# Attention with experts behind it: denominators apart from values, the out projection opened early, the next batch's norm and half of the slots moved

## The chip, the cores and the metric

One core of a Trainium2 chip runs the kernel. Its engines are TensorE (PE: matrix products and transposes), VectorE (DVE), ScalarE (ACT), GpSimd (POOL) and SyncE (SP, which issues most transfers). The metric is the time of one execution on the device in microseconds (us).

## The reference

Cut to what matters. Four batches of 512 tokens, 256 features; 64 context rows each; 16 heads of 16 features; 8 experts with 1024 hidden features, 2 per token.

```python
def xattn(Q, K, V, ...):               # Q = layernorm(x), K = V = context
    q, k, v = Q @ Wq + bq, K @ Wk + bk, V @ Wv + bv          # split into 16 heads
    A = softmax(scale * einsum("blhe,bshe->bhls", q, k))
    return einsum("bhls,bshd->blhd", A, v).reshape(B, L, H * E) @ We + be
x = x + xattn(layernorm(x), context, ...)
def ffn(x, ...):                       # x = layernorm(x)
    probs = softmax(x @ router_w + router_b)
    top_w, top_idx = top_k(probs, 2)
    comb = sum(top_w[..., None] * one_hot(top_idx, E), axis=1)
    for e in range(E):
        out += comb[:, e] * (gelu(x @ up[e].T) @ down[e].T)
x = x + ffn(layernorm(x), ...)
```

## The kernel before, in words

The kernel has two stages. The attention stage takes the batches one after the other and also routes the tokens: for each token it finds two experts and a slot in a table. The expert stage, behind it, gathers rows by that table, multiplies them with the experts' weights and adds them to the output. The change touches the attention stage only.

Products that must keep float32 precision are done in three: the left side and the right side are each split into a high half (ACT copies it, rounded) and a low half (VectorE subtracts the high half from the source), and PE multiplies high by high, high by low and low by high (`three`, L1253). So nearly each product waits for an ACT copy and a VectorE subtraction.

Each engine has its own queue, written out by hand, and executes it in order; semaphores hold it where it needs another's result. An engine's `batch(i)` works on three batches at once: the scores of batch i, the second half of the softmax, the out projection and the router logits of batch i-1, and the slots of batch i-2.

PE's queue for one batch (L1471): values and denominators of heads 0 to 7 of batch i-1 (`values`, four j, L1339); half of batch i's normed rows turned (`x_turn`); turned scores j = 4..7 (`scores_turned`); the other `x_turn`; values and denominators of j = 4..7; `project_q(i)`, first k = 1 and then k = 0; the denominators turned (`den_turn`); counts for the slots (`positions`); scores in four parts with the turned reciprocals (`rden_turn`) and their spread over the features (`spread`) between them; `project_out(i-1)`; the maxima turned (`max_turn`); turned scores j = 0..3; the second norm's rows turned (`x2_turn`); `slots` half 0; router logits; their transpose; `slots` half 1.

`values` writes, for each j, a product of 32 columns into bankA and one into bankB0, in the quarter j % 4 of the output partitions. The profile shows products of different quarters starting within 0.02 us of each other. bankB0 (which is also bank 3 of bankC) serves in turn for the denominators, q (k = 0), the first half of the out projection and the router logits; bankB1 for x_turn, q (k = 1) and the second half of the out projection.

VectorE's queue for one batch (L1001): `norm1` of batch i (normed rows xn); `low01` (low halves of expert weights, two operations); `x_low` half 0; `router` of batch i-2 (probabilities, the two best); `x_low` half 1; `chosen` (masks); `q_low` twice; own counts; `rden_split` (reciprocals of the denominators and their halves); the score maxima in four parts, with `att` (attention output times reciprocal) and `att_low` (its low half, at_l) between them; `max_split`; `ranks` and `count`; `residual_norm2` of batch i-1, which ends with the rows xr; `puts` (eight pairs hot/put for the slots); `logits`.

ACT makes the high halves, the exponentials (`exps`) and copies out of PSUM (`av_copy`, `den_copy`, `x2_turn`, `logit_copy`). POOL makes block forms of the keys (`key_blocks`, L381), four operations per batch that wait for the last turned score; the powers for the norms (`rstd`); and the value blocks.

Behind the loop comes the rest of the last batch: values, slots of batch 2, a few products of zeros (`keep_busy`) between short steps, the out projection and the first expert products. `low01` of the last batch stands on VectorE's queue ahead of `residual_norm2`.

## Time and profile before

| | us |
|---|---|
| median of 3 runs | 405.82 |
| lowest and highest | 405.77, 406.33 |
| the profiled execution | 406.0 |
| its span, first to last instruction | 403.5 |
| PE busy | 370.9 (92%) |
| VectorE busy | 242.4 (60%) |
| ScalarE busy | 180.1 (45%) |
| POOL busy | 159.0 (39%) |
| mean granted clock of PE | 0.988 of full |

Busy times are of one engine each and overlap. A line of the profile gives the engine, the line of the kernel, the tile written and those read, the shape, and in brackets how long the engine was idle before it and what ended the wait. The busy time of matrix products is modelled and includes their overlap with the next, so the distance from start to start says what a product takes: 0.23 us for 512 columns, 0.12 for 256.

### The profile page before, as it was taken

How to read it: one execution, taken by the hardware profiler on the slowest of the kernel's cores; microseconds unless marked ns; L12 is line 12 of the kernel's file. 1: busy time of each engine (PE TensorE's matmuls, PEld its weight loads, DVE VectorE, ACT ScalarE, POOL GpSimd, SP SyncE). 2: the span in 40 equal slices, each digit the busy share in tenths (PEclk: the TensorE clock that was granted, in tenths of full speed). 3: DMA queues.
4: the chain of work that ended last, by engine and by line, in shares of the span. 5: the costliest groups of instructions: out<-in, count | busy, mean ns of one | idle time of the engine just before them, and what ended most of it. 6: DMA issues, size and time to landing. Idle time of an engine off the chain costs nothing.

```text
span 403.5 us, 8452 instructions
## 1 busy us (share of the span) xinstructions
PE 370.9 (92%) x2521; PEld 326.4 (81%) x2522; DVE 242.4 (60%) x693; ACT 180.1 (45%) x283; POOL 159.0 (39%) x186
## 2 busy tenths in 40 slices
PE   8998988998898888989889999999999999999990
PEld 8775667576566656988889999999999999999990
DVE  4267596789979975878334366574747447342440
ACT  1263544444444424643325557465474274262340
POOL 2043402212040204115454683846648718616522
PEclk9999999999999999998999999999999999999996
DMA  8910301041031111155232373937556522312322
GB/s 271 352 72 1 106 0 53 2 158 54 0 105 54 53 55 54 54 155 162 42 57 26 66 226 78 251 92 202 169 105 210 106 25 53 56 23 45 49 24 26
DMA packets 26389, 37.23 MB, mean 92 GB/s; under 512 B 4705, under 2 KB 17441, under 8 KB 26369
## 3 DMA queue, kind: packets, MB, share of 16 engines
q1 hardware_dynamic: 19312, 26.98, 20.2%
q0 software_dynamic: 7056, 9.99, 14.3%
q8 instruction: 11, 0.18, 0.2%
q14 instruction: 10, 0.07, 0.1%
HBM read 27.18 MB, written 9.79 MB: 92 GB/s over the span
## 4 chain that ended last, share of the span: by engine, by line
PE 73%; DVE 15%; issue 5%; POOL 3%; ACT 3%; DMA 1%; DVEq 0%; POOLq 0%; ACTq 0%
PE bankC L1255 10%; PE bankC L1257 10%; PE bankC L1256 10%; PE bankD L1619 7%; PE bankD L1620 6%; PE bankD L1621 6%; DVE nmax L798 3%; PE bankC L1454 3%; PE bankA L1587 2%; PE bankA L1349 2%; PE bankC L1619 2%; PE bankC L1450 2%; PE bankC L1620 1%; PE bankC L1621 1%; POOL rstd L374 1%
## 5 line engine op out<-in xcount | busy, mean ns | idle before, releaser
L700 ACT ACTIVATE hh<-bankC 128x512 fp32r<-128x512 f32 (+1 forms) x52 | 36.3, 697 | 93.3 <-PE bankC L1257 93.3
L1255 PE MATMUL bankC<-xnT_h,up_w 128*128 128x256 f32 (+1 forms) x240 | 74.5, 310 | 2.0 <-ACT prime L694 1.4
L1256 PE MATMUL bankC<-xnT_l,up_w 128*128 128x256 f32 (+1 forms) x240 | 72.9, 304 | 0.0
L1257 PE MATMUL bankC<-xnT_h,up_w 128*128 128x256 f32 (+1 forms) x240 | 72.8, 303 | 0.0
L1619 PE MATMUL bankD<-dn_w,hh 128*128 x208 | 59.9, 288 | 0.9 <-issue 0.5
L1620 PE MATMUL bankD<-dn_w,hh 128*128 x208 | 58.3, 280 | 0.5 <-issue 0.5
L1621 PE MATMUL bankD<-dn_w,hl 128*128 x208 | 58.1, 279 | 0.0
L450 POOL DMA_INDIRECT xr<-rows,idx_g x35 | 47.3, 1353 | 14.8 <-issue 14.0
L1182 DVE TENSOR_TENSOR hl<-prob,hh 128x512 fp32r<-128x512 f32 (+1 forms) x26 | 21.2, 816 | 46.1 <-ACT prob L701 46.1
L1255 PEld LDWEIGHTS bankC<-xnT_h,up_w 128*128 128x128 f32 x240 | 45.5, 190 | 2.9 <-ACT prime L694 1.6
L1256 PEld LDWEIGHTS bankC<-xnT_l,up_w 128*128 128x128 f32 x240 | 45.7, 191 | 0.0
L1257 PEld LDWEIGHTS bankC<-xnT_h,up_w 128*128 128x128 f32 x240 | 45.6, 190 | 0.0
L1619 PEld LDWEIGHTS bankD<-dn_w,hh 128*128 128x128 f32 x208 | 39.0, 188 | 3.6 <-issue 2.8
L1621 PEld LDWEIGHTS bankD<-dn_w,hl 128*128 128x128 f32 x208 | 39.1, 188 | 0.6 <-issue 0.6
L1620 PEld LDWEIGHTS bankD<-dn_w,hh 128*128 128x128 f32 x208 | 39.1, 188 | 0.0
L374 POOL TENSOR_TENSOR rstd<-var,cst 128x2 f32<-128x2 f32 (+2 forms) x10 | 9.6, 958 | 65.2 <-DVE var L862 58.0
L1182 DVE TENSOR_TENSOR hl<-raw,hh 128x512 fp32r<-128x512 f32 (+1 forms) x26 | 21.2, 815 | 23.3 <-ACT raw L701 23.3
L418 POOL TENSOR_TENSOR prime<-prime 1x1 f32<-1x1 f32 x39 | 12.1, 309 | 58.5 <-DVE gate L1169 49.2
L455 POOL DMA_INDIRECT out<-x2T,idx_s x18 | 29.7, 1648 | 6.1 <-issue 6.1
L1255 PE MATMUL bankC<-hh 128*128 128x512 f32 x64 | 26.8, 419 | 3.2 <-ACT nmxT L557 2.8
L566 ACT ACTIVATE prob<-bankC 128x512 f32<-128x512 f32 x32 | 19.1, 598 | 15.3 <-PE bankC L1337 15.3
L455 POOL DMA_INDIRECT out<-av,idx_s x14 | 24.1, 1718 | 3.6 <-issue 3.6
(312 smaller groups left out, 866.9 us busy)
## 6 DMA issues: line engine op xcount, KB each, us to landing
xall<-up SPq DMA_DIRECT2D x24, 256.0 KB, 3.8
xall<-down SPq DMA_DIRECT2D x24, 256.0 KB, 4.2
rows<-xr SPq DMA_DIRECT2D x4, 528.0 KB, 3.3
raw<-up SPq DMA_DIRECT2D x4, 512.0 KB, 4.7
raw<-down SPq DMA_DIRECT2D x4, 512.0 KB, 5.3
out<-xall SPq DMA_DIRECT2D x4, 512.0 KB, 2.8
xall<-x SPq DMA_DIRECT2D x1, 1536.0 KB, 8.2
cst<-const SPq DMA_DIRECT2D x1, 640.0 KB, 8.2
```

What stands on the lines that cost most here:

```text
L374: return g.tensor_tensor(out_, var_, c("power")[:, 0:n], ALU.pow)
L450: return g.indirect_dma_start(xr[:, t, :], None, rows, bass.IndirectOffsetOnAxis(idx_g[:, n:n + 1], 0), bounds_check=T + P - 1)
L455: g.indirect_dma_start(out, bass.IndirectOffsetOnAxis(idx_s[:, n:n + 1], 0), y[ring][:, t, :], None, bounds_check=T + P - 1, compute_op=AL ...
L566: a.activation(prob[:, j % 4, :], bankC[:, j % 3, :], ACT.Exp, scale=SCALE).then_inc(a_exp, 1)
L700: a.activation(hT_h[:, 2 * q:2 * q + 2, 0:n * P], bank, ACT.Gelu)
L1182: v.tensor_tensor(hT_l[:, 2 * q:2 * q + 2, 0:n * P], hbuf[q][:, :, 0:n * P], hT_h[:, 2 * q:2 * q + 2, 0:n * P].bitcast(F32), ALU.subtract) ...
L1255: mm(out_, left_h, right_h, start=first, stop=False)
L1256: mm(out_, left_h, right_l, start=False, stop=False)
L1257: return mm(out_, left_l, right_h, start=False, stop=last)
L1619: mm(out_, hT_h[:, m, o], w_h, start=(m == 0), stop=False)
L1620: mm(out_, hT_h[:, m, o], w_l, start=False, stop=False)
L1621: last = mm(out_, hT_l[:, m, o], w_h, start=False, stop=(m == KF - 1))
```

## The change

All of it is in the order of the queues and in what is waited for; no product and no operation is added or taken away.

- Out projection: the offset products of both halves come first, without a wait for the low half; the high halves follow after a wait for `a_at`, the low halves last after `v_at`.
- Turned scores, j = 0: the wait for the turned maxima moves from ahead of the three score products to ahead of the product that adds the maxima.
- `values` becomes `weighted` and `denominator`. For j = 0..3 the weighted values stand at the end of the batch ahead of the logits, the denominators last; x_turn of the next batch stands between the logits and their transpose. For j = 4..7 they stay together.
- `project_q` k = 1, `den_turn`, `project_q` k = 0; on VectorE `rden_split` between the two `q_low`.
- `norm1` of the next batch stands behind `residual_norm2`, ahead of the first four pairs of `puts`; the other four pairs and their slot products move into the next batch (behind `x_low` half 0, and behind `x_turn` half 1). `low01` moves behind them.
- Behind the loop, `positions` stands between the turned scores, and the last `puts` half of batch 1 is made there.

```diff
@@ ScalarE @@
                     if j >= 4:
-                        act.wait_ge(p_av, 16 * b + 2 * (j - 3))
+                        act.wait_ge(p_av, 16 * b + j + 1)
...
             def av_copy(b, k):
-                act.wait_ge(p_av, 16 * b + 8 * k + 8)
+                act.wait_ge(p_av, 16 * b + 12 * k + 4)
...
             exps(0, range(4))
+            av_copy(0, 0)
+            x_high(1, 0)
             def batch(i):
-                av_copy(i - 1, 0)
-                x_high(i, 0)
                 exps(i - 1, range(4, 8))
...
                 x2_turn(i - 1)
+                av_copy(i, 0)
                 logit_copy(i - 1)
+                if i + 1 < B:
+                    x_high(i + 1, 0)
                 router_exp(i - 1)
@@ VectorE @@
-            def batch(i, with_router):
-                norm1(i)
+            norm1(1)
+            def batch(i):
+                x_low(i, 0)
+                if i >= 3:
+                    puts(i - 3, 1)
                 low01(i - 1)
-                x_low(i, 0)
...
-                q_low(i)
+                q_low(i, (0,))
+                rden_split(i - 1)
+                q_low(i, (1,))
...
-                rden_split(i - 1)
                 maxima(i, 0)
...
                 residual_norm2(i - 1)
-                if with_router:
+                if i + 1 < B:
+                    norm1(i + 1)
+                if i >= 2:
                     puts(i - 2, 0)
-                    puts(i - 2, 1)
                 logits(i - 1)
...
             chosen(B - 2)
+            puts(B - 3, 1)
@@ TensorE @@
-                    if j == 0:
-                        pe.wait_ge(a_nmT, b + 1)
-                        pe.wait_ge(a_const, 4)
...
                     three(bankC[:, j % 3, :], kh, kl, q_h[:, k, :], q_l[:, k, :], True, False)
+                    if j == 0:
+                        pe.wait_ge(a_nmT, b + 1)
+                        pe.wait_ge(a_const, 4)
                     mm(bankC[:, j % 3, :], sel_r[:, j, :], nmxT[:, :], start=False, stop=True).then_inc(p_sT, 1)
...
+            def weighted(b, j):
+                if j == 0:
+                    pe.wait_ge(g_vbd, b + 1)
+                    if b:
+                        pe.wait_ge(a_x2T, 2 * b - 1)
+                pe.wait_ge(a_exp, 8 * b + j + 1)
+                o = slice(32 * (j % 4), 32 * (j % 4) + 32)
+                mm(bankA[o, j // 4, :], vbd[:, j, :], prob[:, j % 4, :], start=True, stop=True).then_inc(p_av, 1)
+            def denominator(b, j):
+                if j == 0 and b:
+                    pe.wait_ge(v_lg, 3 * (b - 1) + 1)
+                o = slice(32 * (j % 4), 32 * (j % 4) + 32)
+                k = j // 4
+                mm(bankB0[o, :], c("densel")[:, 32 * k:32 * k + 32], prob[:, j % 4, :], start=(k == 0),
+                   stop=(k == 1), skip_group_check=True).then_inc(p_av, 1)
...
-                pe.wait_ge(v_at, KD * b + KD)
...
                 for n in range(2):
                     mm(bankB[n][:, :], one_r[:, :], bias_2, start=True, stop=False, skip_group_check=True)
+                for n in range(2):
+                    for k in range(KD):
+                        pe.wait_ge(a_at, KD * b + k + 1)
+                        for h in range(2):
...
                             mm(out_, at_h[:, k, o], we_h[:, k, :], start=False, stop=False, skip_group_check=True)
                             mm(out_, at_h[:, k, o], we_l[:, k, :], start=False, stop=False, skip_group_check=True)
+                    for k in range(KD):
+                        pe.wait_ge(v_at, KD * b + k + 1)
+                        for h in range(2):
+                            o = slice((2 * n + h) * P, (2 * n + h + 1) * P)
+                            last = mm(bankB[n][:, h * D:(h + 1) * D], at_l[:, k, o], we_h[:, k, :], start=False,
+                                      stop=(k == KD - 1), skip_group_check=True)
...
             scores_turned(0, range(4))
+            for j in range(4):
+                weighted(0, j)
+            x_turn(1, 0)
+            for j in range(4):
+                denominator(0, j)
-            def batch(i, router):
-                values(i - 1, range(4))
-                x_turn(i, 0)
+            def batch(i):
                 scores_turned(i - 1, range(4, 8))
                 x_turn(i, 1)
-                values(i - 1, range(4, 8))
-                project_q(i)
+                if i >= 3:
+                    slots(i - 3, 1)
+                for j in range(4, 8):
+                    weighted(i - 1, j)
+                    denominator(i - 1, j)
+                project_q(i, (1,))
                 den_turn(i - 1)
+                project_q(i, (0,))
...
                 scores_turned(i, range(4))
                 x2_turn(i - 1)
-                if router:
-                    slots(i - 2, 0)
+                for j in range(4):
+                    weighted(i, j)
                 logits(i - 1)
+                if i + 1 < B:
+                    x_turn(i + 1, 0)
                 logits_turn(i - 1)
-                if router:
-                    slots(i - 2, 1)
+                if i >= 2:
+                    slots(i - 2, 0)
+                for j in range(4):
+                    denominator(i, j)
...
-            values(B - 1, range(4))
+            scores_turned(B - 1, range(4, 6))
             positions(B - 2, bankB1)
-            scores_turned(B - 1, range(4, 8))
+            scores_turned(B - 1, range(6, 8))
+            slots(B - 3, 1)
             slots(B - 2, 0)
             slots(B - 2, 1)
```

## Rows read from the trace of the kernel before

**Rows 1.** Busy time by stage: length, then busy time and count per engine, clock.

```profile
71.50:105.90 34.40, 30.96 (x188) 22.41 (x188) 30.77 (x99) 14.72 (x25) 6.88 (x8) 1.00 0.18 63
...
162.50:404.00 241.50, 224.86 (x1710) 217.83 (x1709) 124.21 (x320) 114.34 (x171) 123.57 (x139) 0.98 0.40 96
```

**Rows 2.** Waits of PE, 15 to 162.5 us: total, times, longest.

```profile
PE bankC L1380 <- DVE hl L829: 3.6, 4, 0.9
...
PE bankC L1255 <- ACT nmxT L557: 2.8, 4, 0.7
...
PE bankA L1364 <- DVE rdm L818: 2.1, 4, 0.7
```

**Rows 3.** PE in order of time: start, us, instruction, [idle before].

```profile
68.01 1.04 PE L1397 MATMUL bankA<-cst,xr 128*128 128x128 f32 x8
...
73.80 0.47 PE L1255 MATMUL bankC<-hh 128*128 128x512 f32 x1
...
92.47 0.47 PE L1380 MATMUL bankC<-be_r,one_r 128*128 128x512 f32 x1 [0.93 <-DVE hl L829]
...
97.14 0.50 PE L1255 MATMUL bankC<-hh 128*128 128x512 f32 x1 [0.69 <-ACT nmxT L557]
```

**Rows 4.** VectorE in order of time, batch 2 into batch 3.

```profile
84.08 0.75 DVE L790 SCALAR_TENSOR_TENSOR hl<-bankC,bias,hh 128x512 fp32r<-128x512 f32 x1 [0.65 <-ACT hh L552]
...
100.38 1.51 DVE L868 TENSOR_SCALAR xr<-xall,mv,rstd 128x256 f32<-128x256 f32 x2 [0.26 <-POOL rstd L374]
...
105.18 0.33 DVE L963 TENSOR_SCALAR put<-cst,key,val 128x128 fp32r<-128x128 f32 x1
...
106.04 1.37 DVE L774 TENSOR_SCALAR xn<-xall,mv,rstd 128x256 f32<-128x256 f32 x4
...
109.60 0.68 DVE L782 TENSOR_TENSOR xnT_l<-bankD,xnT_h 128x512 fp32r<-128x512 f32 x1
...
110.20 0.17 DVE L888 TENSOR_REDUCE lsum<-ex 128x4 f32<-128x32 f32 x1
...
111.75 0.16 DVE L900 FIND_INDEX8 i<-v,pr 128x8 uint32<-128x8 f32 x1
```

**Rows 5.** PE in order of time, end of batch 2 into batch 3.

```profile
104.07 0.64 PE L1406 MATMUL bankC<-x2T,rw 128*32 128x128 f32 x16
...
105.89 1.08 PE L1349 MATMUL bankA<-prob,vbd 128*32 128x512 f32 x8
...
107.76 0.66 PE L1285 MATMUL bankD<-cst,xn 128*128 128x128 f32 x4
...
108.17 0.47 PE L1255 MATMUL bankC<-hh 128*128 128x512 f32 x1
...
114.64 0.50 PE L1255 MATMUL bankD<-xnT_h,wq_h 128*128 128x512 f32 x1
```

**Rows 6.** PE in order of time, batch 1.

```profile
40.52 0.67 PE L1285 MATMUL bankD<-cst,xn 128*128 128x128 f32 x4 [0.49 <-DVE xn L774]
```

**Rows 7.** VectorE and POOL in order of time, beside and not beside each other.

```profile
80.02 1.02 DVE L907 TENSOR_TENSOR mk<-cst,ef 128x64 f32<-128x64 f32 x1
...
142.73 0.22 DVE L907 TENSOR_TENSOR mk<-cst,ef 128x64 f32<-128x64 f32 x1
...
77.92 2.04 POOL L390 TENSOR_TENSOR hh<-kT_h,cst 128x512 fp32r<-128x512 f32 x2 [10.36 <-PE bankC L1337]
```

**Rows 8.** VectorE in order of time, last batch.

```profile
140.77 0.18 DVE L888 TENSOR_REDUCE lsum<-ex 128x4 f32<-128x32 f32 x1 [0.29 <-ACT ex L597]
...
149.04 0.33 DVE L963 TENSOR_SCALAR put<-cst,key,val 128x128 fp32r<-128x128 f32 x1
```

**Rows 9.** Busy time by stretch, last batch and around the one fall of PE's clock.

```profile
140.20:162.50 22.30, 19.19 (x118) 12.81 (x118) 15.68 (x64) 7.90 (x13) 4.34 (x4) 1.00 0.16 50
...
178.70:181.30 2.60, 1.28 (x7) 0.78 (x6) 2.60 (x14) 1.21 (x3) 1.14 (x1) 1.00 0.92 299
...
182.38:185.80 3.42, 3.42 (x18) 3.42 (x17) 2.03 (x7) 1.09 (x2) 0.57 (x1) 0.50 0.89 284
```

More of the change, by code:

```diff
@@ L648, in _ @@
                 batch(i)
-            av_copy(B - 1, 0)
             exps(B - 1, range(4, 8))
@@ L785, in x_low, with q_low @@
                                     ALU.subtract).then_inc(v_xT, 1)
-            def q_low(b):
-                for n, k in enumerate((1, 0)):
+            def q_low(b, ns):
+                for n in ns:
+                    k = 1 - n
                     dve.wait_ge(a_q, KD * b + n + 1)
@@ L983, in _ @@
                                        op0=ALU.add, op1=ALU.subtract).then_inc(v_k, 1)
-            q_low(0)
+            q_low(0, (0, 1))
             dve.wait_ge(d_const, 16)
@@ L1020, in batch @@
                 max_split(i)
-                if with_router:
+                if i >= 2:
                     ranks(i - 2)
@@ L1024, in batch @@
                 residual_norm2(i - 1)
-                if with_router:
+                if i + 1 < B:
+                    norm1(i + 1)
+                if i >= 2:
                     puts(i - 2, 0)
-                    puts(i - 2, 1)
                 logits(i - 1)
-            batch(1, False)
-            for i in range(2, B):
-                batch(i, True)
+            for i in range(1, B):
+                batch(i)
             router(B - 2)
             chosen(B - 2)
+            puts(B - 3, 1)
             own_counts(B - 2, bankB1)
@@ L1286, in x_turn, with project_q @@
                 last.then_inc(p_xT, 1)
-            def project_q(b):
+            def project_q(b, ks):
                 pe.wait_ge(v_xT, 2 * b + 2)
@@ L1291, in project_q @@
                     pe.wait_ge(v_wsplit, 1)
-                for k in (1, 0):
+                for k in ks:
                     if k == 0 and not (isinstance(b, int) and b == 0):
@@ L1462, in _ @@
                 .then_inc(p_map, 1)
-            project_q(0)
+            project_q(0, (1, 0))
             values_of_two(0)
@@ L1482, in batch @@
                 rden_turn(i - 1)
-                scores(i, 1, router)
+                scores(i, 1, i >= 2)
                 spread(i - 1)
@@ L1490, in batch @@
                 x2_turn(i - 1)
-                if router:
-                    slots(i - 2, 0)
-                logits(i - 1)
-                logits_turn(i - 1)
-                if router:
-                    slots(i - 2, 1)
-            batch(1, False)
-            for i in range(2, B):
-                batch(i, True)
-            values(B - 1, range(4))
+                for j in range(4):
+                    weighted(i, j)
+                logits(i - 1)
+                if i + 1 < B:
+                    x_turn(i + 1, 0)
+                logits_turn(i - 1)
+                if i >= 2:
+                    slots(i - 2, 0)
+                for j in range(4):
+                    denominator(i, j)
+            for i in range(1, B):
+                batch(i)
+            scores_turned(B - 1, range(4, 6))
             positions(B - 2, bankB1)
-            scores_turned(B - 1, range(4, 8))
+            scores_turned(B - 1, range(6, 8))
+            slots(B - 3, 1)
             slots(B - 2, 0)
@@ L1552, in down_early @@
                     last.then_inc(p_de, 1)
-            values(B - 1, range(4, 8))
+            for j in range(4, 8):
+                weighted(B - 1, j)
+                denominator(B - 1, j)
             keep_busy(0, 3)
```

24 lines of the change are left out of this document (4 added, 20 removed).

## The prediction

> **What bounds the kernel now.** I read the page's slices first: TensorE (PE) is 92% busy and near 100% in the expert stage, which the change doesn't touch and which takes 241.5 us [rows 1]. So the change can act only in the attention stage, where a batch takes 34.4 us, 31.0 of it with PE busy and, nearly as much, 30.8 with VectorE busy [rows 1]. The reader should see two engines near their limit, not one. Next, what PE waits for: three waits come back in each of the four batches, for the low half of the attention output (0.9), for the copy of the turned maxima (0.7) and for the turned reciprocals (0.7) [rows 2]. The orders of time then say what stands behind each. PE sits 0.93 before the offset product of the out projection and 0.69 before the first turned scores [rows 3]. VectorE, from its second q_low on, has hardly a gap until the next batch's router is done [rows 4]; what PE saves in that stretch comes through only as far as VectorE delivers the normed rows (xr), on which PE's x2 transposes wait.
>
> I work with the profiled execution: 406.0 us, of which 403.5 are span; the median of the runs is 405.82, so a difference found in the profile is put on 405.82 as it is.
>
> **The change part by part.**
>
> *Out projection opened with offset and high halves.* The same 26 products; two offset (0.24 each) and eight high ones (0.12 each) no longer wait for at_l. They are 1.4 us of work in front of a wait of 0.93 [rows 3], so it goes whole. PE: -0.9 to -1.1 per batch.
>
> *Maxima added after three score products.* Three products of 0.23 fill the 0.69 [rows 3]. PE: -0.7 per batch.
>
> *Reciprocals turned between the two halves of q.* The denominators reach VectorE 1.4 us sooner, and it splits them in the 0.65 us in which it now waits for the second half of q [rows 4]. The second q_low itself comes some 0.5 later, because 0.44 of transposes stand before its products. PE saves 0 to 0.7 [rows 2]; I take 0.6. VectorE's chain, and this counts more, ends between 0.3 and 0.9 sooner; I take 0.6, near the gap of 0.65 that is filled.
>
> *What of it arrives.* PE is now 2.3 us early at the x2 transposes, VectorE's xr only 0.6 (last one at 100.38 + 1.51 = 101.89 before [rows 4]). So of these three edits 0.6 comes through in a full batch, and PE stands idle for most of the rest just ahead of the transposes.
>
> *The tail of a batch.* From the last xr to the first of scores_turned(4..7) it is 108.17 - 101.89 = 6.3 us now [rows 4, 5]. On VectorE stand eight pairs hot/put (0.46 each: 101.89 to 105.18 + 0.33), then the logits; behind them on PE come the four values and four denominators, 107.76 - 105.89 = 1.9, and x_turn, 0.4 [rows 5]. After: VectorE makes the norm of the next batch (1.3, from 106.04 to 107.33), four pairs (1.8), the logit sum (0.2); PE's weighted values (0.95), logits (0.64) and x_turn lie beside that; then four denominators, 0.95 with the change of shape, and 0.2 for hand-overs. Sum 1.3 + 1.8 + 0.2 + 0.95 + 0.2 = 4.45. Gain 1.85. With the 0.6: batch 2 -2.45.
>
> *Batch 1.* Here x_turn waits for the first normed rows, which come from VectorE and POOL at 40.52 whatever PE does [rows 6]. What PE gained before is lost in that wait, and four denominators that ran ahead of it now run behind it: +1.0. VectorE wins this back (0.6, and 0.4 that it waited for PE), so xr comes when it did. PE's x2 transposes, which started late at 68.01 and took 0.9, end 0.8 sooner. From there to 73.80 [rows 3] there are no pairs; the weighted values now cover the wait for the x2T copy, the denominators wait for the logit turn: 4.9 becomes 3.9. Batch 1 in all: -1.8. Start of batch 2's second half of scores: -1.8; of batch 3's: -1.8 - 2.45 = -4.2.
>
> *Entry of batch 3.* The moved second half of the slots stands, on VectorE's queue, ahead of low01, the router and x_low(1), for which project_q waits; on PE ahead of the weighted values. From the start of scores_turned to project_q it is 114.64 - 108.17 = 6.5 [rows 5]. VectorE, from the logit sum: rest of the logits 0.45, x_low 0.6, four pairs 1.8, low01 2.3 (107.33 to 109.60), router 1.7 (110.20 to 111.91), x_low 0.65 [rows 4], 7.7 with the sum's own 0.2. Later the router also meets POOL's key blocks, which start when the turned scores end: a small product of two SBUF tiles took 1.02 beside POOL, as long as one POOL operation, and 0.22 alone [rows 7]. No row shows the router's other operations beside POOL, so this costs 0 to 4.1 (the four POOL operations, 2 x 2.04); I take 0.8, one such meeting. 8.5 from the sum, of which 1.2 lie before the scores start: 7.3, so +0.8. project_q of batch 3: -3.4.
>
> The Trainium skill (SBUF — State Buffer, section "SBUF: two separate sides") says that only VectorE instructions with two SBUF inputs, or in a two-port mode, wait for POOL's, and then for the whole of one. By it one operation of the router is caught, which is the 0.8; without it the cost could run to the 4.1.
>
> *The last batch.* xr: -3.4 - 0.6 = -4.0. Its tail up to the router's first sum (140.77 [rows 8]), 4.5 before from the last xr, becomes 3.8: -4.7. Then VectorE must make the four pairs left over, +1.8: up to the last put (149.04 [rows 8]) -2.9, and a wait of 0.1 on PE goes: -3.0. Behind it, in the chain of latencies through denominators, reciprocals and out projection, nothing changes but the opening of the projection, 0.9; but VectorE's residual is queued behind x_low and 2.3 of low01 and does not start sooner for it, so I count it at 0 (at most -0.9). The expert stage shifts as a whole. Sum -3.0.
>
> *The clock.* This is the cost that the change adds without an instruction. PE's granted clock falls once, from 2.4 to 1.2 GHz, for 3.4 us; before it, PE had been busy 1.28 of 2.60 us while four slot products waited for their pairs [rows 9]. In the changed kernel the score products of the last batch end some 6 us before the last put, and PE has only about 12 small slot products in that time. That is emptier and longer than the stretch that this trace shows before its fall. The four-wide products that follow at once would run at half speed. Cost: 0 if it doesn't fall or falls and rises while PE waits, 1.7 (half of 3.42 [rows 9]) if all of it is exposed; I take 1.1. Result: -3.0 + 1.1 = -1.9, 403.9 us.
>
> The Trainium skill (TensorE: Matmul & The Clock Gate, section "What's actually happening") says that half rate is the default and that activity releases it, so an emptier queue can cost clock; this trace agrees with its one fall to 0.50 [rows 9].
>
> **The rivals.**
>
> *B, no fall of the clock behind the last slots, or the lock does not bite.* For it: the last batch of the kernel before has waiting slots too, and its clock is 1.00 throughout [rows 9]. Then -3.0 to -3.8: 402.8, at best 402.0.
>
> *C, the clock falls inside the batches too.* Waiting is no longer spread over three places but gathered ahead of the x2 transposes, 2.3 idle of 3.2 us in batches 2 and 3. Each fall costs up to 1.7 there, as weighted values, logits, x_turn and denominators follow with under a microsecond of slack. One fall: 405; two: 407 with the full price, slower than before. It decides from the second on. Against: in the kernel before, similar but shorter waits go without a fall. The slower side is this.
>
> *D, VectorE takes the gain.* If more of the router, or the mask operations behind it, are caught by POOL, or low01 holds the key blocks back, project_q of batch 3 comes 2 or more us later; with the clock's 1.1 little is left: 405.4. For it: VectorE's 30.8 of a batch that is to take 32 [rows 1]. It is also the form in which the change doesn't do what it says, moving PE's waits without shortening the batch.
>
> **How the numbers follow.** As worked out 0.5 (402.8 to 405.0), B 0.2, C 0.15, D 0.15. The predicted time is the first's, 403.9. The range reaches from B's upper part to C's first fall: 402.2 to 405.9. A difference below 0.2% (0.8 us) can't be told from none. Faster by more: nearly all of the first, all of B, some of D: 0.78. Same: most of D's rest and C's first fall, 0.12. Slower: C from its second fall, 0.10.
>
> **What would show it.** Right: no wait before the offset product and under 0.1 before the first turned scores; a new wait of 1 to 2 us on xr in batches 2 and 3; x_turn of batch 1 still at 40.5 and the scores behind it 1.0 later; batch 2 shorter by about 2.4 us; the last put near 146.2; and a stretch at clock 0.50 that begins between 143 and 150. Wrong: scores_turned of batch 3 not 3 us earlier than 108.17, which would break VectorE's share; project_q of batch 3 later than 112.5, which is D; more than two stretches at 0.50, which is C.

## The result, and the profile after

The changed kernel takes 403.81 us (median of 8 runs, 402.23 to 404.85), the kernel before beside it on the same chip 405.97 (8 runs): ratio 0.9932, 95% interval 0.9905 to 0.9959. A second series, of 12 runs, gave 403.91 and 0.9942 (0.9914 to 0.9970). The ratio says more than the medians, which differ by 0.5%: two of the eight runs of the kernel before took 407.5 and 408.7, and of its 77 runs beside the experiments 26 lie between 407.6 and 409.9, all with a mean granted clock of 0.985 or less, 50 lie below 407.0, all with 0.986 or more, and one, at 512.4, was slow altogether and is left out. The forecast was 403.9. The total is right; below it stand errors of a microsecond and more that cancel.

The profiled execution took 404.05 us, span 402.1 (before 406.0 and 403.5). Its stages (length; busy and count of PE, PEld, VectorE, ScalarE, GpSimd; clock), to be held against [rows 1]:

```profile
71.50:103.27 31.77, 30.12 (x186) 21.42 (x182) 28.91 (x93) 14.84 (x25) 6.86 (x8) 1.00 0.20 67
160.71:402.00 241.29, 223.03 (x1710) 214.97 (x1708) 125.08 (x321) 114.46 (x171) 124.75 (x139) 0.99 0.40 96
```

A batch from the start of its second half of scores to the next one's is 2.6 us shorter, and PE's 30.1 now fill 95% of it. VectorE's busy time fell by 1.9: four pairs of hot and put (1.8) have left this batch for the next one's entry, with their slot products. The waits of PE from 15 to 162.5 us (total, times, longest) [rows 2]:

```profile
PE bankA L1415 <- DVE xr L871: 3.2, 7, 0.6
PE bankD L1462 <- DVE put L966: 2.5, 4, 2.0
PE bankD L1293 <- DVE xn L776: 2.0, 1, 2.0
...
PE bankA L1377 <- DVE rdm L821: 0.4, 1, 0.4
...
PE bankD L1263 <- DVE xnT_l L784: 0.3, 1, 0.3
```

The wait for the low half of the attention output (3.6) and the one for the maxima (2.8) are gone, that for the reciprocals is down from 2.1 to 0.4. Of the 8.1 that have gone from these three, 3.2 stand in one new place, xr. In order of time on PE [rows 3, 5, 6]:

```profile
40.47 0.67 PE L1293 MATMUL bankD<-cst,xn 128*128 128x128 f32 x4 [2.04 <-DVE xn L776]
41.07 1.06 PE L1363 MATMUL bankC<-prob,cst 128*32 128x512 f32 x8
42.07 0.50 PE L1263 MATMUL bankC<-hh 128*128 128x512 f32 x1
...
66.33 0.92 PE L1415 MATMUL bankA<-cst,xr 128*128 128x128 f32 x6
...
71.51 0.50 PE L1263 MATMUL bankC<-hh 128*128 128x512 f32 x1
...
96.77 0.76 PE L1415 MATMUL bankA<-cst,xr 128*128 128x128 f32 x4 [0.58 <-DVE xr L871]
98.17 0.44 PE L1415 MATMUL bankA<-cst,xr 128*128 128x128 f32 x2 [0.64 <-DVE xr L871]
98.86 0.44 PE L1415 MATMUL bankA<-cst,xr 128*128 128x128 f32 x2 [0.25 <-DVE xr L871]
...
103.27 0.50 PE L1263 MATMUL bankC<-hh 128*128 128x512 f32 x1
...
110.23 0.50 PE L1263 MATMUL bankD<-xnT_h,wq_h 128*128 128x512 f32 x1 [0.30 <-DVE xnT_l L784]
```

The first three rows show the price at the start: x_turn waits 2.04 for xn, as before at 40.5, and four denominators that had run ahead of it run behind. At 96.77 to 98.86 PE waits 1.47 in three pieces: it arrives early, as forecast, and has to stand. The signs that the prediction named are all there: no wait before the offset product, none before the first turned scores, and this one on xr. VectorE and POOL at the entry of batch 3 [rows 4, 7]:

```profile
97.30 1.50 DVE L871 TENSOR_SCALAR xr<-xall,mv,rstd 128x256 f32<-128x256 f32 x2 [0.27 <-POOL rstd L374]
...
107.47 1.03 DVE L895 TENSOR_TENSOR pr<-ex,lrec 128x32 f32<-128x32 f32 x1
108.54 0.17 DVE L899 MAX8 v<-pr 128x8 f32<-128x8 f32 x1
...
110.51 1.02 DVE L910 TENSOR_TENSOR mk<-cst,ef 128x64 f32<-128x64 f32 x1
```

```profile
107.40 2.04 POOL L390 TENSOR_TENSOR hh<-kT_h,cst 128x512 fp32r<-128x512 f32 x2 [8.75 <-PE bankC L1345]
109.41 2.05 POOL L390 TENSOR_TENSOR hl<-kT_l,cst 128x512 fp32r<-128x512 f32 x2
```

One router operation with two SBUF inputs lies in POOL's block and takes 1.03 (0.19 alone, in the last batch); MAX8 and the index searches beside the same block keep their 0.16 to 0.17. That is the one meeting of 0.8 that the sum had, and the rule of the Trainium skill on which kind of instruction waits (SBUF — State Buffer, "SBUF: two separate sides") agrees. The mask operation (mk, 1.02) is no new cost: it lay beside POOL before too, 1.02 at 114.39. The one behind it (msum_bf) lies outside the block now, 0.19 at 111.57 for 0.93 at 115.45 before. The end of the attention, PE, and its clock (windows as above) [rows 8, 9]:

```profile
140.72 0.56 PE L1462 MATMUL bankD<-put,hot 128*128 128x128 f32 x4
143.29 0.30 PE L1462 MATMUL bankD<-put,hot 128*128 128x128 f32 x1 [2.01 <-DVE put L966]
...
144.65 2.25 PE L1462 MATMUL bankD<-put,hot 128*128 128x128 f32 x5 [0.15 <-DVE put L966]
146.70 0.23 PE L1537 MATMUL bankD<-seen_bf,ones_bf 128*128 128x8 bf16 x1
146.86 1.96 PE L1355 MATMUL bankA<-prob,vbd 128*32 128x512 f32 x8
148.57 1.95 PE L1363 MATMUL bankC<-prob,cst 128*32 128x512 f32 x8
...
151.74 0.60 PE L1370 MATMUL bankA<-cst,den 128*128 128x128 f32 x4
...
157.42 0.39 PE L1392 MATMUL bankC<-be_r,one_r 128*128 128x512 f32 x1
```

```profile
131.05:134.46 3.41, 3.36 (x26) 1.28 (x26) 1.80 (x8) 1.20 (x2) 0.00 (x0) 0.50 0.00 0
144.70:151.53 6.83, 6.76 (x25) 2.98 (x26) 2.04 (x10) 0.75 (x2) 2.79 (x3) 0.50 0.10 27
```

The fall behind the last slots came where it was forecast (between 143 and 150), but for 6.83 us, and it lies over the four weighted values and four denominators too (two records each), which take 1.96 and 1.95 for the 1.07 and 1.06 that they have at full clock. And there is a second one at 131 that the forecast's main case did not have. The one fall of the kernel before, at 182 [rows 9], is missing.

### The profile page after: what moved, and what is told of

The parts are those of the page before. It is cut to its first block, busy times and chain, and to the rows that moved or that the text cites. A ratio compares the mean times of both kernels' runs of the same rounds, so it can differ in the third digit from the quotient of the medians.

```text
span 402.1 us, 8455 instructions
## 1 busy us (share of the span) xinstructions
PE 372.2 (93%) x2521; PEld 323.3 (80%) x2522; DVE 241.8 (60%) x693; ACT 180.4 (45%) x283; POOL 160.1 (40%) x186
## 4 chain that ended last, share of the span: by engine, by line
PE 69%; DVE 18%; issue 6%; POOL 4%; ACT 2%; DMA 1%; DVEq 0%; POOLq 0%; ACTq 0%
PE bankC L1263 10%; PE bankC L1264 9%; PE bankC L1265 9%; PE bankD L1651 7%; PE bankD L1652 6%; PE bankD L1653 6%; DVE nmax L801 3%; PE bankC L1472 3%; PE bankA L1355 2%; POOL rstd L374 2%; PE bankA L1619 2%; PE bankC L1651 2%; PE bankC L1468 2%; PE bankC L1652 1%; PE bankC L1653 1%
```

## The experiments

Two executions of one kernel can start their products up to 1 us apart and have falls of the clock ("falls": stretches at a granted clock of 0.50) in other places, so positions below are counted from the turn of batch 0's maxima (32.14 in the kernel before, 32.09 in the changed one), which every kernel has at the same point of its work. The second execution of the changed kernel is after_again. Columns: project_q of batches 2 and 3, second half of scores of batch 3 (3b) and of the last batch (4b; in the kernel before it stands behind the positions, so it has no comparable value), product of the total count, first product of the early experts, end of the span; all in us.

```
                    q2     3b     q3     4b     total   expert  end     falls (start, length)
before              48.12  76.03  82.50  -      117.51  130.41  371.37  150.2 3.4
changed             45.91  71.18  78.14  104.51 114.61  128.62  369.97  99.0 3.4; 112.6 6.8
after_again         45.89  71.19  78.15  103.11 113.22  126.76  368.58  110.4 6.8
opening_undone      46.86  72.16  79.13  104.11 114.22  129.35  369.99  112.7 6.8
both_waits_back     47.58  72.90  79.86  104.85 114.97  129.64  370.60  112.0 6.8; 149.6 3.4
split_undone        46.81  73.99  80.98  107.94 118.10  132.18  373.79  68.9 3.4; 103.0 3.4; 116.7 6.8
norm_undone         48.31  73.72  82.09  107.05 117.17  131.17  372.71  9.8 3.4; 115.6 6.8
puts_undone         45.93  74.05  81.04  109.29 119.08  132.29  374.31  71.7, 102.5, 109.3, 119.5: 3.4 each
waits_filled        46.28  71.59  78.55  103.68 113.64  127.09  372.09  110.3 6.8; 147.8 3.4
fill_last_slots     45.92  71.22  78.18  103.15 113.44  125.21  370.16  154.7 3.4; 171.8 3.4
first_den_ahead     44.75  70.05  77.01  101.99 112.11  125.67  367.56  109.4 6.8
last_values_ahead   45.91  71.19  78.18  104.44 114.44  126.77  367.72  99.2 3.4; 119.7 3.4
two_ahead           44.71  70.00  76.96  101.92 111.93  122.96  363.43  none
tail_rearranged     44.69  71.03  78.01  102.97 112.98  123.25  364.79  65.7 3.4; 113.5 3.4
```

Falls within 12 us of the end of the span are left out.

**The changed kernel again.** No edit.

> The changed kernel once more, with no edit: how much of a profile is the kernel's and how much this execution's. Theory (where the granted clock falls is not fixed to an instruction; between executions a fall of 3.4 us may be missing or stand elsewhere): places up to the start of the x2 transposes of batch 3 within 0.3 us of 129.01 unless a fall lies ahead of them, and then later by about 1 to 1.7 per fall; one to three falls. Rival (the falls belong to fixed places): falls again at 131 and at 144.7, all positions within 0.1.

403.91 us, 0.9942 (0.9914 to 0.9970). Up to 3b the two executions agree within 0.02. The fall at 99 is not there, and from there on all stands 1.4 earlier. So whether a fall comes inside the batches, and where, is not fixed by the kernel alone, and this is what one costs; the one behind the last slots came in both. The execution without it is the rarer one: the mean clock of the 20 runs of the changed kernel is 0.977 to 0.985, this profile has 0.985 and the first one 0.981, and one fall of 3.41 is worth 0.004; so most of the others, by this estimate, have at least one fall more than this profile.

**The opening of the out projection.**

```diff
                 pe.wait_ge(v_one, 4)
+                pe.wait_ge(v_at, KD * b + KD)
...
-                    for k in range(KD):
-                        pe.wait_ge(a_at, KD * b + k + 1)
-                        for h in range(2):
+                    for h in range(2):
+                        for k in range(KD):
...
```

> The changed kernel with the out projection as before (waits for the whole low half, offset per half). Theory (VectorE decides): the wait of 0.9 comes back four times, but in batches 2 and 3 it is taken out of the idle time ahead of the x2 transposes (now 1.5 us there), which start and end as in the changed kernel; only batch 1, with 0.25 idle, gives 0.6 later. Time +0.6, 404.4. Rival (TensorE decides): +0.9 in each batch, 406.5 or more.

404.37 us, 0.9918 (0.9886 to 0.9951): the time doesn't tell it from the changed kernel. Positions do: q2 is 0.97 later, and 3b, q3, 4b and the total stand 0.97 to 1.00 later, not 2 or 3 times that. The opening is worth its 0.9 in batch 1 and nothing in batches 2 and 3. PE's x2 transposes there, with the old wait of 0.93 in front of them again:

```profile
98.15 0.60 PE L1410 MATMUL bankA<-cst,xr 128*128 128x128 f32 x4
99.13 0.44 PE L1410 MATMUL bankA<-cst,xr 128*128 128x128 f32 x2 [0.38 <-DVE xr L871]
99.82 0.44 PE L1410 MATMUL bankA<-cst,xr 128*128 128x128 f32 x2 [0.25 <-DVE xr L871]
```

The last pair starts 0.97 later than in the changed kernel, all of it from batch 1; the wait on xr has shrunk from 1.47 to 0.63 and paid for the rest. That is more than the 0.6 that the run's theory had. In the last batch the offset product comes 2.5 later than in the second execution of the changed kernel, 1.5 of them at den_turn already and 1.0 from the opening itself; but the end of the span is only 1.4 later, so the 1.0 doesn't reach it.

**Opening and maxima wait both back.** The edit above, and

```diff
-                    three(bankC[:, j % 3, :], kh, kl, q_h[:, k, :], q_l[:, k, :], True, False)
                     if j == 0:
                         pe.wait_ge(a_nmT, b + 1)
                         pe.wait_ge(a_const, 4)
+                    three(bankC[:, j % 3, :], kh, kl, q_h[:, k, :], q_l[:, k, :], True, False)
```

> The changed kernel with the out projection's old order (nothing starts before all of the attention output and its low half are there) and with the wait for the turned maxima ahead of the first three score products. Theory (PE had 1.5 us of idle ahead of the x2 transposes in batches 2 and 3, 0.2 to 0.5 in batch 1; the opening alone used 0.9 of it): batch 1 longer by 1.3 to 1.6 (project_q of batch 2 at 79.3 to 79.6, was 78.00), batches 2 and 3 by 0 to 0.3 each, total product at 146.9 to 148.5, time 404.3 to 405.5. Rival (the two waits are paid in full in each of the four batches, 1.6 each): total product at 151 or later, time above 408.

404.89 us, 0.9956 (0.9930 to 0.9982). q2 is 1.69 later, and it stays at 1.7 to 1.75 down to the total. Waits of 6.4 us (3.6 and 2.8) are back on PE in four batches, and 1.7 of them arrive up to the total: the two of batch 1, 0.93 and 0.7. The theory stands, with 0.1 more in batch 1 than its 1.3 to 1.6: in batches 2 and 3 these two edits of three move a wait.

**The reciprocals' place.**

```diff
                 project_q(i, (1,))
-                den_turn(i - 1)
                 project_q(i, (0,))
+                den_turn(i - 1)
...
                 q_low(i, (0,))
-                rden_split(i - 1)
                 q_low(i, (1,))
                 if i >= 2:
                     own_counts(i - 2, bankC[:, 2, :])
+                rden_split(i - 1)
```

> The changed kernel with both halves of q projected before the denominators are turned, and the reciprocals split after both low halves, as before. Theory (VectorE decides): its chain up to xr gets 0.6 longer in each of batches 1 to 3 and TensorE's idle time ahead of the x2 transposes grows by nothing; last put 1.8 later than 146.3, time 405.6. Rival (TensorE's wait of 0.7 is eaten by idle time elsewhere): last put within 0.3 of 146.3, time 403.8.

408.11 us, 1.0011 (0.9981 to 1.0042): the whole gain of the change is gone without this one edit. Before any fall, q2 is 0.92 later. VectorE's xr comes 1.71 later in batch 2 and 3.63 later in batch 3, both ahead of the fall of their batch, and the project_q before them 0.92 and 2.83 later: 0.8 in each. So the 4.88 at the total are 2.5 of its own and 2.4 of the two falls. The forecast had 0.6, the expectation 1.8 in all. That the time is more than 2.5 higher (4.2 between the medians, 2.8 to 3.2 by the ratios) fits falls too: all 12 runs have a mean clock of 0.973 to 0.978. Why this order has more of them is open.

**The next norm's place.** On VectorE norm1(i + 1) moved behind logits(i - 1), with x_high and x_turn behind the router's exponential and the denominators:

```diff
                 residual_norm2(i - 1)
-                if i + 1 < B:
-                    norm1(i + 1)
                 if i >= 2:
                     puts(i - 2, 0)
                 logits(i - 1)
+                if i + 1 < B:
+                    norm1(i + 1)
```

> The changed kernel with the norm of the next batch, its x_high and its x_turn back behind the logits; the puts stay split between batches. The prediction's sum for a batch's tail has the norm (1.3) in both orders, so the norm's place is worth 0 and only the four pairs that left the tail are worth 1.8. Theory: scores(4..7) of batches 2 and 3 start within 0.5 per batch of 71.5 and 103.3, time within 0.2% of the changed kernel (403 to 404.7). Rival: the early norm hides x_turn and the first half's turn copies as well; then each of three tails is 0.8 to 1.3 longer, last total product at 149 to 150.5 instead of 146.7 and the time 406 to 407.5.

406.73 us, 0.9989 (0.9963 to 1.0014), so my theory for this run fell: the norm's place is worth more than 2 us, near what its rival said. The execution has a fall at 9.8, and project_q of batch 1 comes at 18.00 for 16.47; less these 1.53, q2 is 0.9 later, 3b 1.0, q3 2.4, the total 2.4. So the tail of batch 2 grows by 0.1 only; the loss lies at project_q, 0.9 in batch 2 and 1.4 in batch 3. VectorE in batch 3's entry:

```profile
103.68 0.19 DVE L880 TENSOR_TENSOR lg<-bankC,rb 128x32 f32<-128x32 f32 x1 [1.01 <-PE bankC L1430]
...
104.23 1.38 DVE L776 TENSOR_SCALAR xn<-xall,mv,rstd 128x256 f32<-128x256 f32 x4
106.36 0.69 DVE L784 TENSOR_TENSOR xnT_l<-bankD,xnT_h 128x512 fp32r<-128x512 f32 x1 [0.75 <-ACT xnT_h L546]
```

and PE at project_q of that batch:

```profile
113.82 0.50 PE L1263 MATMUL bankD<-xnT_h,wq_h 128*128 128x512 f32 x1 [1.72 <-DVE xnT_l L784]
```

The sum of VectorE's work is the same in both orders. What differs is that two latencies come bare: the logit turn, which the norm covers (1.01), and the way of the norm over PE and ScalarE back to x_low (0.75). Together they are 1.76, and PE's wait at project_q has grown by 1.42, from 0.30 to 1.72. A sum of durations doesn't show an order's worth; the idle times do.

**The pairs of hot and put.** The second four and their slot products back at the end of a batch:

```diff
                 x_low(i, 0)
-                if i >= 3:
-                    puts(i - 3, 1)
...
                     puts(i - 2, 0)
+                    puts(i - 2, 1)
...
```

> The changed kernel with the second four hot/put pairs and their slot products back at the end of a batch, behind the first four; the norm stays early. Theory: the tail of batches 2 and 3 is longer by 1.8 each (scores(4..7) of batch 3 at 105.1 instead of 103.27), project_q of batch 3 is then 0 to 0.5 later (its entry is shorter by the 1.8 and by the meeting of the router with POOL), and the last batch has no leftover pairs, -1.8: last total product at 146.5 to 147.5, time 403.5 to 405, that is, moving the pairs gains next to nothing over the kernel, since what leaves a tail comes back in an entry or at the end. Rival (the prediction's sum, in which they leave two tails and return once, and the entry costs only 0.8 net): total product 1.0 later or more, 147.7 to 149, time 405 to 406.

408.73 us, 1.0033 (1.0003 to 1.0064). 3b is 2.87 later; the rows of PE and the clock there:

```profile
102.57 0.30 PE L1460 MATMUL bankD<-put,hot 128*128 128x128 f32 x1 [0.15 <-DVE put L966]
...
103.93 0.45 PE L1460 MATMUL bankD<-put,hot 128*128 128x128 f32 x1 [0.15 <-DVE put L966]
104.30 1.93 PE L1361 MATMUL bankC<-prob,cst 128*32 128x512 f32 x8
```

```profile
103.85:107.26 3.41, 3.33 (x12) 1.39 (x13) 3.34 (x7) 0.23 (x1) 0.00 (x0) 0.50 0.00 0
```

Four pairs, 1.8, and the rest, 1.05, the clock's fall (the denominators take 1.93 for 1.06). q3 is 2.89 later. In the entry PE no longer has the four slot products and its idle 0.30, which gives 0.5 back, and the end of the fall, under the first scores, takes 0.5 again (from the first of them to x_turn it is 4.30 instead of 3.80). More doesn't come back, since PE sets the entry and not VectorE; the theory of the run fell there. The rival's size (1.0 or more at the total) is passed by far: 5.9, with three falls inside the batches, the third under the last scores. At the 1.05 to 1.5 that a fall costs in these runs, 1.4 to 2.7 are left for the pairs; this run doesn't say it nearer. As without the reciprocals' place, the clock is lower in all 12 runs, 0.968 to 0.978.

**Zero products ahead of the x2 transposes.** `keep_busy(1, 2)` issues two products of zeros.

```diff
                 for n in range(2):
+                    if not (isinstance(b, int) and b == B - 1):
+                        if n == 0:
+                            pe.wait_ge(a_exp, 8 * (b + 1) + 2)
+                        keep_busy(1, 2)
                     for t in range(2):
                         pe.wait_ge(v_xn2, LT * b + 2 * n + t + 1)
```

> The changed kernel with two products of zeros (0.47 us together) in front of each pair of x2 transposes of batches 1 to 3, where TensorE waits 0.5 to 0.6 for the normed rows; they change no result. Theory (the fall at 131 comes from the emptier stretch at the x2 transposes, and costs about 1 where products follow that set the end): no fall between 125 and 137, the first turned scores of the last batch at 135.3 to 135.9 instead of 136.60, the fall behind the last slots stays, time 402.5 to 403.8. Rival (the fall at 131 is accidental, or the zero products delay the transposes): scores at 136.5 or later, time 403.5 to 405.

406.37 us, 0.9984 (0.9957 to 1.0011), slower than the changed kernel beside it (403.91; 12 runs each). In the attention stage the zero products cost 0.4 in batch 1, and 4b is later than in the second execution of the changed kernel, which has no fall at 99 either: nothing was to be won. The rest of the loss, 3.2, lies behind the first expert product, with a fall at 148 and an idle time of 1.9 in the down products; why, is not settled.

**Zero products between the last slots.**

```diff
             slots(B - 3, 1)
-            slots(B - 2, 0)
-            slots(B - 2, 1)
+            pe.wait_ge(a_exp, 8 * B)
+            keep_busy(0, 7)
+            for q in range(8):
+                slot(B - 2, q)
+                keep_busy(0, 1)
```

> The changed kernel, with zero products put into the wait of the last batch's slots (seven before the first of batch 2's slot products, one behind each of the eight), nothing else. Theory (the price is the clock): no stretch at 0.50 between 138 and 158 us; the last put as in the changed kernel (near 146.3), the denominators turned near 149.8 instead of 151.7; time 1.2 to 2.2 us below the changed kernel's 403.8. Rival (latencies of ScalarE and VectorE cover the slow stretch): turned near 149.8 too, but the first expert product (160.7 now) not more than 0.5 sooner, time 403.5. Second rival (zero products delay the slots): last slot product later than 146.9, time 404 or more.

404.93 us, 0.9929 (0.9901 to 0.9957).

```profile
146.53 0.18 PE L1543 MATMUL bankD<-seen_bf,ones_bf 128*128 128x8 bf16 x1
146.64 1.08 PE L1355 MATMUL bankA<-prob,vbd 128*32 128x512 f32 x8
147.52 1.06 PE L1363 MATMUL bankC<-prob,cst 128*32 128x512 f32 x8
```

The fall behind the slots is gone and the values have their full rate; the eight profiles of other kernels and executions that have 6.83 there leave the slots' waits empty. From the total to the first expert product it is 11.77 instead of 13.54 (14.01 in the first execution), and all of it lies ahead of den_turn: the fall costs 1.8. But the time didn't follow, and the theory's 1.2 to 2.2 fell: the span ends 1.6 later than in the second execution of the changed kernel, with two falls and a wait of 2.19 on VectorE's low halves in the expert stage. Two kernels with zero products added to the attention stage had, from the first expert product to the end, 245.0 where the changed kernel has 241.4 and 241.8. What joins the two is open.

**Batch 0's denominators ahead of the first x_turn.**

```diff
-            x_turn(1, 0)
             for j in range(4):
                 denominator(0, j)
+            x_turn(1, 0)
```

> The changed kernel with batch 0's four denominators ahead of the first x_turn of batch 1, where TensorE is idle for 2.0 us. Theory: turned scores start at 41.0 instead of 42.07 and all that follows up to the last put comes 0.9 to 1.0 sooner (145.3), unless the norm's xr of batch 1 waits elsewhere; time 402.8. Rival (the loss was made good before batch 2 anyway): start of batch 2's scores (71.5) unchanged, time 403.8.

402.73 us, 0.9879 (0.9835 to 0.9923), six runs; the interval overlaps that of the changed kernel, so the positions have to tell. q2, 3b, q3, 4b and the total are 1.1 earlier, and so is the first expert product. The cost at the start was real and was passed on whole.

**The last batch's values ahead of the slots.**

```diff
+            for j in range(4, 8):
+                weighted(B - 1, j)
+                denominator(B - 1, j)
             slots(B - 2, 0)
+            den_turn(B - 1)
             slots(B - 2, 1)
...
-            for j in range(4, 8):
-                weighted(B - 1, j)
-                denominator(B - 1, j)
-            keep_busy(0, 3)
-            den_turn(B - 1)
-            keep_busy(0, 4)
+            keep_busy(0, 7)
```

> The weighted values and denominators of the last batch's second half, and the turning of its denominators, stand ahead of the slot products of the batch before instead of behind them; the same instructions otherwise. Theory (the attention of the last batch waits for nothing that the slots give, it only stands behind them in PE's queue): the total of the counts still starts at 146.7 +- 0.6, den_turn, at 151.74 in the changed kernel, moves to before 143, and the out projection of the last batch starts 3 to 6 us earlier than 157.42, bounded by VectorE, which has the pairs and low01 in front of the residual; the expert stage starts 2 to 4 us sooner than 160.71, time 400 to 402. Rival 1 (VectorE's queue sets the residual whatever PE does): out projection earlier, but the first expert product less than 1 us earlier; time 403.8. Rival 2 (the expert stage's own state, not its start, sets the end, as one run with a fuller tail suggested): first expert product 2 to 4 us earlier, end less than 1 us earlier, and the stage from there to the end longer than 239 instead of 236.7.

401.92 us, 0.9847 (0.9803 to 0.9891). den_turn starts at 144.93 for 151.74, and PE's queue had been what held the denominators, as the theory says; but the out projection starts only 1.65 earlier, at 155.77, and the first expert product 1.64, less than its 2 to 4, and den_turn isn't before 143. A new wait has taken the place,

```profile
149.78 0.72 PE L1385 MATMUL bankA<-rdT,feat_r 128*128 128x512 f32 x2 [0.22 <-ACT rdT L578]
152.61 1.11 PE L1549 MATMUL bankC<-cst,ctxT 128*128 128x128 f32 x4 [2.10 <-DMA ctxT<-rows,se]
```

the gather of the early experts' rows, which waits for the last slot product (146.60) and is there 6.0 behind its start. Not all of the gain is the queue's: the values and denominators no longer stand behind the slots, where the clock fell for 6.83 us. two_ahead, which has no fall, reaches the first expert product 2.7 earlier than first_den_ahead, which has that one; at the price of fill_last_slots 1.8 of the 2.7 would be the clock's and 0.9 the queue's. No run separates the two.

**Both ahead, and then the tail rearranged.** First the last two edits together; then besides

```diff
             spread(B - 1)
-            x_turn_early(0, bankC[:, 2, :])
             keep_busy(0, 6)
-            project_out(B - 1)
+            project_out(B - 1, (0,))
+            x_turn_early(0, bankC[:, 2, :])
+            project_out(B - 1, (1,))
```

with the two subtractions of low01(B - 1) one ahead of att and one behind att_low.

> The changed kernel with batch 0's denominators ahead of the first x_turn of batch 1, and the last batch's second half of weighted values and denominators, and their turn, ahead of the slots of the batch before. Alone they gave 1.1 and 1.9 to 3.4 us. Theory (one acts at the start, the other at the end, so they add): first expert product at 157.9 to 158.3 (160.71 in the changed kernel), time 399.5 to 401.5. Rival (the gather of the early experts' rows, which waits for the last slot product and lands 5.9 us behind it, already sets the end of the attention and moves with the pairs, or the expert stage takes the gain in waits for its own DMAs): time 401.5 or more.

> The same as the kernel with both parts ahead, and besides: in the last batch the first half of the out projection stands in front of the transposes of the gathered rows (for which TensorE waited 2.10 with nothing else to do), the second half behind them, and the two low-half subtractions of the weights fill VectorE's gaps of 2.0 ahead of the attention output and of 1.3 ahead of the gathered rows' low half. Theory: the out projection starts at 150.5 to 152 instead of 155.8, the first expert product at 154 to 156, time 396.5 to 399. Rival (the gain is given back at the x2 transposes, whose normed rows come 5.4 after the residual starts, or at the expert stage's DMAs): time 399.5 to 401, with a wait of 1 to 2.5 on xr or on a DMA.

399.68 us, 0.9834 (0.9789 to 0.9880), and 398.48 us, 0.9797 (0.9748 to 0.9845). The first lies in its theory's range (its profiled execution had no fall at all and took 397.7). The second's time lies in its theory's 396.5 to 399 too, but that theory counted from 155.8, and two_ahead already had the out projection at 151.99 and the first expert product at 155.27. Against these the second brought the out projection forward by 1.3 and the first expert product by 0.8, once its fall inside the batches is allowed for with the 1.05 by which q3 is later (its second fall, at 113.5, is not allowed for); the 1.2 between the medians lie within the width of the intervals, so that the rearrangement itself shortens the time is not shown. Both kernels are faster than the changed one beyond their intervals.

## Why the prediction was right, and where it was not

*The opening, the maxima, the reciprocals.* Right in kind: of the three only VectorE's share arrives in a full batch. The share is 0.8 (split_undone, batches 2 and 3), not 0.6, and nothing of PE's (both_waits_back: 1.69 at q2, 1.75 at the total). I had taken the middle between 0.3 and 0.9; it is near the upper end. PE's idle time ahead of the x2 transposes is 1.5 in batch 2; the prediction's 2.3 early less 0.6 would be 1.7.

*Batch 1.* The start was sized right (+1.1 for +1.0). But PE, not VectorE, set this batch, so opening and maxima arrive there, 1.7 (both_waits_back). The second half of scores of batch 2 started at 39.42 behind the turn of the maxima for 41.66, a gain of 2.2; forecast 1.8.

*Tail and batch 2.* Forecast -2.45, measured 34.37 to 31.77, -2.6. The tail was priced well, for the pairs that left it: the norm's place moves it by 0.1 only (norm_undone). The sum counts the norm's 1.3 in either order and gives its place nothing; norm_undone has 0.9 and 1.4 for it, at the project_q of batches 2 and 3.

*Entry of batch 3.* +0.5 for +0.8, with the one meeting on pr. The entry's sum of durations without idle time holds because the early norm covers the latencies that norm_undone lays bare. project_q stands 4.4 earlier; forecast 3.4.

*The last batch.* The router's sum came at 136.20, 4.57 earlier (forecast 4.7), the last put at 145.98, 3.06 earlier (forecast 2.9). These hits are luck: the profiled execution carries a fall at 99 that costs 1.4 and that the sum did not have (the first of rival C's). Without it the total stands 4.3 earlier. The term "3.0 up to the last put" was 1.3 too small, 0.45 of it from batch 1, 0.15 from batch 2, 0.3 from the entry; 0.4 lie in the last batch, where VectorE's larger share accounts for 0.2.

*The clock.* The mechanism was right, and its place. The size, 1.1, was not: counted from the total, fill_last_slots is 1.8 shorter up to den_turn and up to the first expert product alike (in position 1.55, 117.94 against 116.39, since its total is 0.2 later), because the fall lies over the values and denominators, on the path, not over waits. Even the 1.7 that the prediction gave as the most was for 3.42 us; this fall has 6.83. Rival C's fall inside a batch appears in most executions, if the mean clocks are read rightly, at 1.05 to 1.5 each.

*Behind the attention.* The opening in the last batch was counted as 0, because VectorE's residual is queued behind low01. That was right. At the offset product the opening gives 1.0 (den_turn stands 2.5 earlier in the second execution, the offset product 3.6), and the first expert product is 3.65 earlier; but VectorE's first addition of the residual stands 2.5 earlier, no more (position 127.15 for 129.68), and at the x2 transposes PE now waits for what comes of it. First the kernel before, then the second execution of the changed one:

```profile
166.76 1.04 PE L1397 MATMUL bankA<-cst,xr 128*128 128x128 f32 x8
```

```profile
164.47 0.77 PE L1415 MATMUL bankA<-cst,xr 128*128 128x128 f32 x4 [0.22 <-DVE xr L871]
165.47 0.76 PE L1415 MATMUL bankA<-cst,xr 128*128 128x128 f32 x4 [0.24 <-DVE xr L871]
```

From there on the changed kernel stays about 2.8 earlier, 2.8 at the end, so the expert stage does shift as a whole, from its x2 transposes on. A wait further on is longer than before, and costs nothing:

```profile
PE bankA L1587 <- DMA xr<-rows,idx_g: 0.7, 1, 0.7
```

```profile
PE bankA L1619 <- DMA xr<-rows,idx_g: 1.7, 1, 1.7
```

The kernel before has its one fall, at 150.2, ahead of this wait. Under the fall the distance between the two kernels grows from 2.7 to 4.1, and behind the wait it is 2.7 again: the gathered rows come when they come, and PE's slow stretch is taken up there.

Put together for the second execution: 4.3 at the total for 3.0, the clock 1.8 for 1.1, a rest of 0.3, which no run places, and 2.8 at the end for 1.9. A fall inside the batches takes 1.4 of this again, as in the first execution, whose end is 1.4 earlier than that of the kernel before. The medians lie between the two, at 2.0 to 2.2. So the hit on the total, 403.9 for 403.8, is a gain sized too small, a price sized too small and a fall that the main case left out.

## What to carry to other kernels

A wait that is removed from an engine shows up in time only where that engine is the late one; find, for each batch, who waits at the next meeting point, and price the edit there: here two edits on PE's waits brought 1.7 of 6.4, and two on VectorE's chain (the reciprocals' and the norm's place), each undone alone, cost 2.4 to 2.5 and left nothing of the gain. An order that gives the same sum of durations can still be 2 us apart through the latencies it leaves bare. And before a position in one profile is taken for the kernel's, look for a fall of the clock ahead of it, or profile twice; the mean clock of the other runs tells which of two profiles is the usual one.

## What the runs showed of the hardware

Apart from the end of the span, the granted clock fell to half (1.2 GHz) for 3.41 or 6.83 us and for no other time, 25 times in 14 profiles. Ahead of several of these falls PE waited between small products (from 101.30 to 103.90 in puts_undone it was busy 1.90 of 2.60 us), and ahead of none was it idle for longer than 2.2 us at a stretch in the last 7 us; but the same stretch of the changed kernel, the one ahead of 131, was followed by a fall in one execution and by none in the other. A fall of 3.41 cost 1.05 to 1.5 inside the batches, one of 6.83 behind the last slots 1.8, and one of 3.41 ahead of a wait for gathered rows nothing. Products of zeros between the last slots went with a profile without the fall there, and did not shorten the kernel.
